# Splat attention logits: one fp32 product against two accumulating fp16 products over stacked high and low parts, with new work on GpSimd and ScalarE

## What is computed

```python
q_dists = jnp.sum((q[:, :, :, None, :] - centers[None, None]) ** 2, axis=-1)
k_dists = jnp.sum((k[:, :, :, None, :] - centers[None, None]) ** 2, axis=-1)
q_weights = jnp.exp(q_dists * inv_var)
k_weights = jnp.exp(k_dists * inv_var)
logits = jnp.einsum('bihs,bjhs,hs->bijh', q_weights, k_weights, amplitudes)
attention = jax.nn.softmax(logits / temp, axis=2)
out = jnp.einsum('bijh,bjhd->bihd', attention, v).reshape(Bx, Tx, Dx)
return out @ out_w.T
```

## Time and profile before

| | |
|---|---|
| time, median of 3 runs | 1561.97 us (1561.53 to 1562.64) |
| profiled execution, first to last instruction (span) | 1559.2 us |
| splat attention in it: first features to the last logits | 344.0 to 937.4 us |
| one slot of it, logits(b, 1) to logits(b+1, 1) | 18.11 us |
| busy in the span: PE, DVE, ACT, POOL | 92%, 77%, 63%, 31% |

### The profile page before, as it was taken

One profiled execution on the slowest core, in us unless ns is written; L12 is line 12 of the kernel. 1 busy time (PEld: TensorE's weight loads), 2 busy tenths in 40 slices (PEclk: granted clock), 3 DMA queues, 4 the chain that ended last, 5 costly groups with the idle time before them and its releaser, 6 DMA issues. The chain is left out here.

```text
span 1559.2 us, 43825 instructions
## 1 busy us (share of the span) xinstructions
PE 1429.5 (92%) x14386; PEld 1030.4 (66%) x14387; DVE 1206.5 (77%) x2666; ACT 981.7 (63%) x1482; POOL 487.1 (31%) x726
## 2 busy tenths in 40 slices
PE   1699999978999999999999997999999799799697
PEld 1499999954666666666666655999999544588343
DVE  8688888847787888787888764888888698588795
ACT  5366666533666666666666654666665399577597
POOL 6321221211222222222222202212212198344585
PEclk9999999987999999999999998999999899899899
DMA  5000000000000000000000000000000000000011
GB/s 237 1 1 0 0 0 0 0 1 1 2 2 2 1 0 0 0 0 0 0 0 1 2 2 2 1 0 0 0 0 0 1 0 1 1 1 0 8 47 54
DMA packets 9528, 14.41 MB, mean 9 GB/s; under 512 B 368, under 2 KB 8560, under 8 KB 8688
## 3 DMA queue, kind: packets, MB, share of 16 engines
q1 hardware_dynamic: 9456, 13.44, 2.4%
HBM read 9.25 MB, written 4.19 MB: 9 GB/s over the span
## 5 line engine op out<-in xcount | busy, mean ns | idle before, releaser
L1311 DVE TENSOR_REDUCE neg_max<-splat_fill_ps 128x2 f16<-128x512 f32 x512 | 333.8, 691 | 91.6 <-PE splat_fill_ps L1090 87.6
L1236 ACT ACTIVATE splat_probs<-splat_ring 128x1024 f32<-128x1024 f32 x256 | 248.1, 1021 | 97.9 <-PE splat_ring L1117 97.9
L875 ACT ACTIVATE zones_b_hidden<-zones_b_hidden_ps,gelu_scale 128x1024 f32<-128x1024 f32 x96 | 107.0, 1114 | 86.0 <-PE zones_b_hidden_ps L805 84.6
L875 ACT ACTIVATE zones_a_hidden<-zones_a_hidden_ps,gelu_scale 128x1024 f32<-128x1024 f32 x96 | 106.9, 1113 | 85.7 <-PE zones_a_hidden_ps L805 84.4
L1117 PE MATMUL splat_ring<-splat_queries,splat_keys 32*128 32x256 f32 x2048 | 152.6, 392 | 4.1 <-ACT splat_probs L1236 3.2
L1090 PE MATMUL splat_fill_ps<-splat_keys,splat_queries 32*128 32x256 bf16 x1024 | 146.6, 279 | 6.1 <-DVE neg_max L1311 3.2
L1131 PE MATMUL splat_mixed_ps<-splat_probs,values 128*32 128x256 f32 x2048 | 137.0, 385 | 0.4 <-ACT splat_probs L1236 0.4
L924 DVE SCALAR_TENSOR_TENSOR zones_a_hid_lo<-zones_a_hidden,unit_scale,zones_a_hid_hi 128x1024 f16<-128x1024 f32 x96 | 123.6, 1288 | 3.4
L924 DVE SCALAR_TENSOR_TENSOR zones_b_hid_lo<-zones_b_hidden,unit_scale,zones_b_hid_hi 128x1024 f16<-128x1024 f32 x96 | 123.6, 1288 | 3.4
L133 POOL TENSOR_TENSOR splat_ended_shifted<-splat_ended_moments,eps 128x2 f32<-128x2 f32 x32 | 6.2, 195 | 344.5 <-DVE splat_ended_moments L127 344.5
L1117 PEld LDWEIGHTS splat_ring<-splat_queries,splat_keys 32*128 32x128 f32 x2048 | 99.6, 184 | 11.2 <-ACT splat_probs L1236 4.0
(11 more groups left out here) (369 smaller groups left out, 3503.4 us busy)
## 6 DMA issues: line engine op xcount, KB each, us to landing
x_res<-rows SPq DMA_DIRECT2D x4, 1024.0 KB, 19.0
out<-x_res SPq DMA_DIRECT2D x16, 256.0 KB, 2.3
stage_a<-wa SPq DMA_DIRECT2D x1, 2048.0 KB, 8.9
stage_b<-wb SPq DMA_DIRECT2D x1, 2048.0 KB, 13.3
packed<-table SPq DMA_DIRECT2D x1, 840.0 KB, 4.5
```

The lines of the kernel that those rows point to most:

```text
L875: nc.scalar.activation(hidden[k][:, :, :], hidden_ps[of][:, :, :], ACT.Gelu_apprx_tanh, scale=s.gelu_scale[:, :]).then_inc(gelu_done, 1)
L1236: nc.scalar.activation(probs[u % PROB_BUFFERS][:, :, :, :].rearrange("p h k i -> p (h k) i"), ring[u % 2][:, :, :], ACT.Exp).then_inc(exp_ ...
L1311: nc.vector.tensor_reduce(s.neg_max[:, tile, t:t + 2, GROUP * g + SPLATS], fill_ps[f % 2][:, :, :], AX.X, ALU.max, negate=True).then_inc(m ...
```

## The change

The features are kept in fp16 and in two parts, a value rounded to fp16 and what the rounding left. The 16 rows of a head that were unused now hold the splats a second time (`feature_w` and `wide_consts` are written for both 16-row halves). On ACT, `keep_features` runs four exponentials in place of two: `wide_keys` (fp32), `const_keys` (fp16, its lower rows made constants by a per-row scale and bias), `high_queries` (fp16) and `wide_queries` (fp32). On POOL, a new `split` makes `lower_keys` (a row mask times `wide_keys`), `keys` (`wide_keys` less that) and `low_queries` (`wide_queries` less `high_queries`). `logits` is now two fp16 products that add up in PSUM, `keys` with `high_queries` and `const_keys` with `low_queries`. `fills` uses `lower_keys` and `high_queries`. `shift` works on `low_queries`. `queries_kept` now follows the last of the four exponentials, and PE waits for it where it waited for `keys_kept`. Apart from this, the copy of the values (`keep_values`) moves from DVE to ACT, between `exps(b, 2)` and `exps(b, 3)`.

```diff
 def logits(b, at, t):
     if t == 0:
+        pe.wait_ge(keys_split, b + 1)
         pe.wait_ge(shifted, TILES * (b + 1))
     if t == 2 and there(b, 2):
-        pe.wait_ge(keys_kept, b + 3)
+        pe.wait_ge(queries_kept, b + 3)
...
-                last = nc.tensor.matmul(ring[g // 2][:, 2 * (g % 2) + key_tile, :],
-                                        keys[at][rows, t, key_tile * P:(key_tile + 1) * P],
-                                        queries[at][rows, t, :], start=True, stop=True)
+        own = slice(key_tile * P, (key_tile + 1) * P)
+        for n, (weight, source) in enumerate(((keys, high_queries), (const_keys, low_queries))):
+            for g in range(HEAD_GROUPS):
+                rows = head_rows(g)
+                last = nc.tensor.matmul(ring[g // 2][:, 2 * (g % 2) + key_tile, :],
+                                        weight[at][rows, t, own], source[at][rows, t, :],
+                                        start=(n == 0), stop=(n == 1))
...
 def fills(b, at, numbers):
...
-            pe.wait_ge(keys_kept, b + 1)
+            pe.wait_ge(queries_kept, b + 1)
+            pe.wait_ge(keys_lower, b + 1)
...
 def keep_features(b, at):
     act.wait_ge(features_done, b + 1)
-    nc.scalar.activation(queries[at][:, :, :], ring[0][:, :, :], ACT.Exp).then_inc(queries_kept, 1)
-    nc.scalar.activation(keys[at][:, :, :], ring[1][:, :, :], ACT.Exp).then_inc(keys_kept, 1)
+    wait(act, keys_split, b)
+    nc.scalar.activation(wide_keys[:, :, :], ring[1][:, :, :], ACT.Exp).then_inc(keys_kept, 1)
+    nc.scalar.activation(const_keys[at][:, :, :], ring[1][:, :, :], ACT.Exp,
+                         bias=s.one_then_none[:, :], scale=s.upper_rows[:, :])
+    nc.scalar.activation(high_queries[at][:, :, :], ring[0][:, :, :], ACT.Exp)
+    wait(act, queries_split, b)
+    nc.scalar.activation(wide_queries[:, :, :], ring[0][:, :, :], ACT.Exp).then_inc(queries_kept, 1)
...
 (ACT) def slot(b, at):
         exps(b, 2)
+    if there(b, 1):
+        keep_values(b + 1, (at + 1) % DEEP)
+    if own:
         exps(b, 3)
...
 (DVE) def slot(b, at):
-        maxima(b + 1, (8, 9, 10))
-        keep_values(b + 1, after)
-        maxima(b + 1, (11,))
+        maxima(b + 1, (8, 9, 10, 11))
...
 (POOL)
+def split(b, at):
+    pool.wait_ge(keys_kept, b + 1)
+    nc.gpsimd.tensor_tensor(lower_keys[at][:, :, :], wide_keys[:, :, :],
+                            s.lower_rows[:, 0:1].unsqueeze(2).to_broadcast([P, FTILES, TOKENS]),
+                            ALU.mult).then_inc(keys_lower, 1)
+    settle(pool, keys_lower, b + 1)
+    nc.gpsimd.tensor_tensor(keys[at][:, :, :], wide_keys[:, :, :], lower_keys[at][:, :, :],
+                            ALU.subtract).then_inc(keys_split, 1)
+    pool.wait_ge(queries_kept, b + 1)
+    nc.gpsimd.tensor_tensor(low_queries[at][:, :, :], wide_queries[:, :, :],
+                            high_queries[at][:, :, :], ALU.subtract).then_inc(queries_split, 1)
```

More of the change, by code:

```diff
@@ L594, in _ @@
                 for g in range(HEAD_GROUPS):
[L595 to L599, removed]
+                    for rows in (slice(0, SPLATS), slice(SPLATS, GROUP)):
+                        nc.vector.tensor_scalar(s.feature_w[:, :, g, rows], small[:, LINEAR:SQUARE + 1, :],
+                                                in_group[:, g:g + 1], None, ALU.mult)
+                        for k, kind in enumerate((QUERY_CONST, KEY_CONST)):
+                            last = nc.vector.tensor_scalar(wide_consts[:, k, g, rows], small[:, kind, :],
+                                                           in_group[:, g:g + 1], None, ALU.mult)
                 last.then_inc(wide_ready, 1)
@@ L975, in splat_attention @@
         square = sb(stage + "_square", [P, 2, TOKENS], F32)
-        queries, keys = ([sb(f"{stage}_{n}{i}", [P, FTILES, TOKENS], F32) for i in range(DEEP)]
-                         for n in ("queries", "keys"))
+        high_queries, low_queries, keys, const_keys, lower_keys = (
+            [sb(f"{stage}_{n}{i}", [P, FTILES, TOKENS], F16) for i in range(DEEP)]
+            for n in ("high_queries", "low_queries", "keys", "const_keys", "lower_keys"))
+        wide_queries, wide_keys = (sb(f"{stage}_{n}", [P, FTILES, TOKENS], F32) for n in ("wide_queries", "wide_keys"))
         probs = [sb(f"{stage}_probs{i}", [P, 2, TILES, TOKENS], F32) for i in range(PROB_BUFFERS)]
@@ L1090, in fills @@
                             last = nc.tensor.matmul(fill_ps[f % 2][:, n, :],
-                                                    upper(queries[at], rows, t + n, slice(tile * P, (tile + 1) * P)),
-                                                    upper(keys[at], rows, t + n, slice(0, TOKENS)),
-                                                    start=True, stop=True)
+                                                    high_queries[at][rows, t + n, tile * P:(tile + 1) * P],
+                                                    lower_keys[at][rows, t + n, :], start=True, stop=True)
                         last.then_inc(fill_done, 1)
@@ L1251, in keep_linear, with keep_values @@
                                          ACT.Copy).then_inc(linear_kept, 1)
+                def keep_values(b, at):
+                    act.wait_ge(values_done, b + 1)
+                    nc.scalar.activation(s.values[:, at, :, :, 0:HEAD_DIM],
+                                         misc_ps[:, 0:TOKENS].rearrange("p (t h c) -> p t h c", t=TILES, h=HEADS),
+                                         ACT.Copy).then_inc(values_kept, 1)
                 def keep_parts(b, half):
@@ L1314, in shift @@
                 def shift(b, at, tile):
+                    dve.wait_ge(queries_split, b + 1)
                     dve.wait_ge(negmax_turned, TILES * b + tile + 1)
-                    rows = queries[at][:, :, tile * P:(tile + 1) * P]
-                    nc.vector.tensor_tensor(rows, rows, misc_ps[:, :].rearrange("p (t i) -> p t i", t=FTILES),
-                                            ALU.add).then_inc(shifted, 1)
+                    rows = low_queries[at][:, :, tile * P:(tile + 1) * P]
+                    nc.vector.scalar_tensor_tensor(rows, rows, s.upper_rows[:, :],
+                                                   misc_ps[:, :].rearrange("p (t i) -> p t i", t=FTILES),
+                                                   ALU.mult, ALU.add).then_inc(shifted, 1)
                 def share(b, half):
@@ L1407, in slot @@
                         apply(b + 3, at)
+                    if there(b, 2):
+                        split(b + 2, (at + 2) % DEEP)
                     if there(b, -2):
```

32 lines of the change are left out of this document (13 added, 19 removed).

## The result

The changed kernel takes 1668.22 us (1662.63 to 1669.12, 4 runs), beside 1562.31 for the kernel before: a ratio of 1.0669 (95% interval [1.0653, 1.0686]; later ratios are given the same way, each to the kernel before). The direction was forecast, the size was not: 106 us more, where 58 were forecast and the range ended at 1646. The profiled execution has a span of 1667.1 us.

What follows compares the result with a forecast made beforehand. PE's own list and the PE-to-ACT chain through one shared buffer were taken as tied bounds. 56.7 + 4.0 - 4.1 + 1.8 = 58.4 us on a 1559.2 span gave 1617.6, median 1620, range 1588 to 1646.

Steps and rivals of the forecast that it cites:

- The chain: Splat stage: PE's products and ACT's exponentials use one buffer in turn, 18.11 us a slot, tied with PE's list.
- its two new waits: PE would wait on ACT some 1.4 us before the first features and some 1.8 before logits t=2.
- The prices: Per-operation costs: logits 0.55 us, exponentials 0.75 after the first product, feature exponentials 0.92 each more, `const_keys` 0.18 extra, POOL 2.12.
- The slot at the full clock: Five legs of a splat-stage slot summed to 20.00 us for 18.11, 1.89 more in each of 30 slots.
- One sign: On ACT, the second exponential of t=1 would start 2.5 us or more after the end of the first.
- Rival one: Splat stage: PE is the bound and the buffer used in turn has slack; faster, 1498 us; 5 in 100.
- rival two: On ACT, the values come early enough and their copy costs 0.33 us alone; 32 us less, 1588; 10 in 100.
- Rival three: On PE, fp16 logits gain nothing because weight loads are not hidden; slot 21.53 us, time 1670; 6 in 100.
- rival four: PE's clock falls to 1.2 GHz as it stands still twice a slot; some 14 us a slot, near 1980; 2 in 100.
- The sum: Whole kernel: 56.7 + 4.0 - 4.1 + 1.8 = 58.4 us more on a span of 1559.2.
- the clock of the stage under 1.00: Splat stage: a granted PE clock below 1.00 would show the forecast wrong; no size given.
- 56.7 - 4.1: Splat stage: 1.89 us more in each of 30 slots, less 8 x 0.51 for logits in two slots without features.

Runs made afterwards that it cites:

- the copy alone: Kernel before, with only the values' copy moved from DVE to ACT between the two exponentials of t=1: 1637.05 us; 1603.46 with 7 unused products ahead of the features.
- the filled kernels: Kernels with unused products added where PE waits: on the changed kernel 1633.01 us, with its values' copy later 1593.61, on the kernel before with the copy moved 1603.46.
- the changed kernel with fillers: Changed kernel plus products that nothing reads on PE, 7 ahead of the first features and 13 ahead of logits t=2: 1633.01 us.
- the later copy of the values: Changed kernel with the values' copy on ACT moved behind both exponentials of t=1: 1619.59 us; 1593.61 with 13 unused products ahead of logits t=2.
- the kernel with two readings: Changed kernel with the values' copy behind both t=1 exponentials and two of four feature exponentials replaced by work from copies already written: 1556.9 us.

## Why the prediction was wrong

**Right, and confirmed.** The chain, its two new waits and their causes: PE waits 1.07 us ahead of the features (forecast 1.4) and 1.79 ahead of logits t = 2 (1.8), ACT 1.61 ahead of the values (1.7). The prices: logits 0.55 us (0.55), `const_keys` 1.20 (1.02 + 0.18), the exponentials 0.73 after the first product (0.75), POOL 1.9 to 2.1 and hidden. The slot at the full clock: 20.07 against 20.00. One sign was off: the second exponential of t = 1 starts 1.90 us after the end of the first (726.91 + 1.05 to 729.86), not 2.5 or more. Rival one (PE is the bound) fails on the waits that PE now has; rival two (the values don't hold ACT) on the 41.5 us of the copy alone. Rival three (the logits gain nothing) fails on the rows: four rounds start 717.34, 717.46, 717.57, 717.68, 0.11 us apart. The Trainium skill, "TensorE: Matmul & The Clock Gate", section "The mechanism" of Part 3, says that a weight load overlaps with a running product only where the row group differs, and also that a load into the background weight buffer is pulled ahead. By the first alone a group's second round would have to wait for its first; the rows, 0.11 us from round to round, do not show such a wait.

**The step that failed** is rival four, *the clock falls*. The forecast judged the clock by a busy share: 16.1 of 20 us, beside a stretch of before that was busy 16.33 and kept 1.00; and it priced the fall as all or nothing, a whole stage at the lower level, at 2 in 100. PE's busy time came out as forecast where the clock held (16.38 of 20 us in 480 to 500), and it was the wrong number. The sum had no term for the clock, and the clock of the stage under 1.00, which the forecast itself named as a sign that it was wrong, came. Shown by the filled kernels: the granted clock drops for a part of most slots, after PE's waits. On the changed kernel that is worth 1668.22 - 1633.01 = 35.2 us, a third of the whole loss, and it should have stood in the sum as a term of 0 to 2 us a slot. Without it the time, 1633.01, lies in the range.

**A smaller term** was sized wrong too. Without the clock's loss in the loop, the kernel is 70.7 us above before, where 58.4 were forecast. The tile's first and last times place it. In the changed kernel with fillers the logits run from 375.5 to 1008.0 us, 632.5, and before from 369.3 to 937.4, 568.1: 64.4 more, where the sum had 56.7 - 4.1 = 52.6. Up to the first logits it is 30.0 us from the first features (345.5) and was 25.3 (344.0): 4.7 more, forecast 4.0, with 1.5 from the set-up, forecast 1.8. So about 12 us belong to the run of slots, and the two traces place most of them, measured from logits t = 1 to the next in the thirty slots with features. Before, such a slot takes 17.99 us on average; the 18.11 of the forecast were read off one of the longer ones, which makes 3.6 us. With fillers, the first two slots take 22.64 and 21.35 us, and the other twenty-eight 20.13 on average where 20.00 were forecast: 3.7 and 3.9 us. The fillers don't reach the first slots, where the clock was still 0.50 to 0.91 up to 420 us and before was back at 1.00 from 380 on. That fits the first two; that the clock alone makes them long is not shown.

## What to carry to other kernels

When a change makes a full PE stand still, price the clock as a term of its own: the duration of the products behind the new wait at both levels, once in most slots, and on the chain if something waits for those products. Measure it by filling the wait with products that nothing reads, at places where PE has nothing to do; the difference is the clock's share, as long as the fillers end before the wait does. A buffer that is used strictly in turn should be read as seldom as possible: what can be made from a copy that is already out need not stand in that chain. Here that was worth 36.7 us, and together with the later copy of the values it turned the change from slower to a little faster. It is not free where the new instruction stands ahead of another that somebody waits for: moving one of the two behind that gave 9 us more.

## What the hardware showed

One wait of 1.06 us a slot was enough to take the granted clock to 0.91 in a stretch where PE was busy 18.91 of 20 us, while the kernel with two readings kept 1.00 with waits of up to 0.79 us and PE busy 18.1 of 20; these are two cases, and no rule follows from them. Products that do nothing made the kernel 35 us faster. And filling one of two such waits made it slower, 1679.77 against 1668.22 us: the slow stretch then met the features in 24 of 30 slots and not in 19, and the fillers held up some logits.
